# Tiles of the first two heads loaded in two steps, fourteen rows ahead of the last chunk's first write and two rows behind its last

## The reference, cut to what matters

```python
q, k, v = h @ wq.T, h @ wk.T, h @ wv.T             # per pixel, 512 -> 512 each
qkv = concat([q, k, v])                            # 1536 channels
dw = conv(qkv, dw_kernel, 5 x 5, one filter per channel)
pw = conv(dw, pw_kernel, 1 x 1, groups of 8 channels)
f = concat([qkv, pw]).reshape(B, 128, 24, N)       # 64 plain heads and 64 convolved ones
query, key, value = relu(f[:, :, :8]), relu(f[:, :, 8:16]), f[:, :, 16:]
scores = einsum('bhdn,bhen->bhde', value with a row of ones, key)
out = einsum('bhde,bhen->bhdn', scores, query)     # then divided by its last row
y = proj(out) * scale + shift + x
```

## Time and profile before

| | |
|---|---|
| median of 3 runs | 4719.41 us (4719.28 to 4723.08) |
| the profiled execution | 4729.61 us, of which 4727.8 us span |
| PE busy | 4394.5 us, 93% of the span |
| DVE, ACT, POOL busy | 2851.6, 2212.0, 1244.8 us |
| mean granted TensorE clock | 0.967 of full speed |
| attention (the phases described above) | about the first 2958 us of the span |

### The profile page before, as it was taken

One profiled execution on the slowest core, in us unless ns is written; L12 is line 12 of the kernel. 1 busy time (PEld: TensorE's weight loads), 2 busy tenths in 40 slices (PEclk: granted clock), 3 DMA queues, 4 the chain that ended last, 5 costly groups with the idle time before them and its releaser, 6 DMA issues. The chain is left out here.

```text
span 4727.8 us, 82817 instructions
## 1 busy us (share of the span) xinstructions
PE 4394.5 (93%) x30440; PEld 3543.8 (75%) x30440; DVE 2851.6 (60%) x4120; ACT 2212.0 (47%) x3983; POOL 1244.8 (26%) x1030
## 2 busy tenths in 40 slices
PE   8999999999999999999999999589989999999968
PEld 6887888888878878878888888466666676666626
DVE  4354454354454454544544544289789978978996
ACT  3343343343343433433433433056576666666666
POOL 2442432433433424424324333000030020002003
PEclk9999999999999999999999999799999999999989
DMA  6685685686776766856866767767456746746613
GB/s 195 222 290 200 234 289 203 240 274 214 245 241 222 265 226 235 285 199 234 288 205 225 265 218 236 267 213 246 163 197 216 248 145 209 253 158 203 204 54 126
DMA packets 486710, 1046.33 MB, mean 221 GB/s; under 512 B 40624, under 2 KB 94512, under 8 KB 484016
## 3 DMA queue, kind: packets, MB, share of 16 engines
q1 hardware_dynamic: 486320, 1040.99, 65.4%
HBM read 665.02 MB, written 375.82 MB: 220 GB/s over the span
## 5 line engine op out<-in xcount | busy, mean ns | idle before, releaser
L825 POOL TENSOR_TENSOR toeplitz<-taps 128x512 f32<-128x512 f32 x768 | 900.7, 1201 | 882.8 <-PE bank L488 804.0
L488 PEld LDWEIGHTS bank<-toeplitz,columns 128*128 128x128 f32 x8192 | 960.4, 193 | 15.1
L488 PE MATMUL bank<-toeplitz,columns 128*128 128x128 f32 x8192 | 960.1, 276 | 0.0
L394 PE MATMUL bank<-x_hi,w_hi 128*128 128x512 f32 x1536 | 619.0, 403 | 19.8 <-DVE x_lo L672 19.2
L396 PE MATMUL bank<-x_lo,w_hi 128*128 128x512 f32 x1536 | 603.9, 393 | 0.0
L395 PE MATMUL bank<-x_hi,w_lo 128*128 128x512 f32 x1536 | 603.9, 393 | 0.0
L1548 POOL TENSOR_TENSOR centred<-centred,x_out 128x512 f32<-128x512 f32 x128 | 174.4, 1384 | 1606.5 <-ACT centred L1331 1604.8
L759 DVE TENSOR_SCALAR ckey_t<-bank 128x256 f32<-128x256 f32 x256 | 108.6, 424 | 776.3 <-PE bank L488 776.3
L1181 PE MATMUL bank<-edge,w_branch 128*128 128x512 f32 x1024 | 485.8, 624 | 76.2 <-ACT edge L1279 76.2
L478 PE MATMUL bank<-loaded,toeplitz 128*128 128x256 f32 x2048 | 505.5, 391 | 53.6 <-DMA loaded<-tiles_dram 45.2
L672 DVE TENSOR_TENSOR x_lo<-x_sb,x_hi 128x1536 fp32r<-128x1536 f32 x128 | 251.8, 1967 | 426.6 <-ACT x_hi L543 426.6
(11 more groups left out here) (143 smaller groups left out, 6836.1 us busy)
## 6 DMA issues: line engine op xcount, KB each, us to landing
x_sb<-in_x_tiled SPq DMA_DIRECT2D x128, 1024.0 KB, 6.2
loaded<-tiles_dram SPq DMA_DIRECT2D x256, 433.5 KB, 5.8
tiles_dram<-tiles SPq DMA_DIRECT2D x112, 867.0 KB, 7.3
inverse<-inverse_dram SPq DMA_DIRECT2D x256, 256.0 KB, 7.9
att_dram<-out_hi SPq DMA_DIRECT2D x256, 256.0 KB, 4.4
att_dram<-out_lo SPq DMA_DIRECT2D x256, 256.0 KB, 5.7
att_hi<-att_dram SPq DMA_DIRECT2D x64, 1024.0 KB, 7.6
att_lo<-att_dram SPq DMA_DIRECT2D x64, 1024.0 KB, 10.0
```

Of the source, the lines that this page charges most:

```text
L394: nc.tensor.matmul(banks[t][:, :], wh, xh, start=(k == 0), stop=False)
L488: last = nc.tensor.matmul(bank[:, v * M:(v + 1) * M], columns[:, h % 2, t - T_K, v + b, a * HT:(a + TO) * HT], w[:, t, d, :], start=(d == ...
L825: last = nc.gpsimd.tensor_tensor(toeplitz[:, h % 2, t, :].rearrange("p (d o r) -> p d o r", o=HD, r=PL), tap, point, ALU.mult)
```

## The change

For heads 0 and 1 of each iteration (`EARLY_HEADS = 2`) the load is split by rows. Rows 0 to 13 (chunks 0 to 6) are loaded ahead of the last chunk's first write, behind a wait for the writes of all chunks up to the seventh (`load_early`). Rows 14 and 15 follow behind the last chunk's last write, each row of each head as a transfer of its own, since a row lies on 8 neighbouring partitions. For this the partitions of `loaded` are in the order (row, channel) in place of (channel, row), for all heads, and the taps are transposed on the host to match. The wait behind the last write is now for one semaphore. The spill that stood between the last write and the loads stands behind the loads. The two waits for a loaded head count the added transfers (`tile_loads`).

```diff
+        EARLY_HEADS = 2
+        FINAL = range(PL - PL // NCH, PL)
+
+        def tile_loads(it, h):
+
+            extra = len(FINAL) if h % LR < EARLY_HEADS else 0
+            return 16 * (SH // LR + extra) * it + 16 * (extra + h // LR + 1)
...
-                def load_head(h):
-
-                    sp.dma_start(loaded[:, h % LR, :, :].rearrange("p t s -> p (t s)"),
-                                 dram["tiles"][h * HD:(h + 1) * HD].rearrange("i r n -> (i r) n")
+                def load_head(h, of):
+
+                    sp.dma_start(loaded[of.start * HD:of.stop * HD, h % LR, :, :].rearrange("p t s -> p (t s)"),
+                                 dram["tiles"][h * HD:(h + 1) * HD, of, :].rearrange("i r n -> r i n")
                                  ).then_inc(tiles_loaded[h % LR], 16)
+
+                def load_early(it):
+                    for n in range(TB):
+                        writes = 1 if n == buffer(NCH - 1) else tile_writes(n)
+                        sp.wait_ge(tile_written[n], 16 * START + 16 * tile_writes(n) * it + 16 * writes)
+                    for h in range(EARLY_HEADS):
+                        load_head(h, slice(0, FINAL[0]))
...
+                        if j == NCH - 1:
+                            load_early(it)
                         write_tiles(it, j)
-                        if conv_of is not None and j >= LATE:
+                        if conv_of is not None and LATE <= j < NCH - 1:
                             spill(conv_of, 1, j - LATE)
...
-                    for n in range(TB):
-                        sp.wait_ge(tile_written[n], 16 * START + 16 * tile_writes(n) * (it + 1))
-
-                    for h in range(LR):
-                        load_head(h)
+                    n = buffer(NCH - 1)
+                    sp.wait_ge(tile_written[n], 16 * START + 16 * tile_writes(n) * (it + 1))
+
+                    for h in range(EARLY_HEADS):
+                        for r in FINAL:
+                            load_head(h, slice(r, r + 1))
+                    for h in range(EARLY_HEADS, LR):
+                        load_head(h, slice(0, PL))
+                    if conv_of is not None:
+                        spill(conv_of, 1, NCH - 1 - LATE)
...
-                    pe.wait_ge(tiles_loaded[h % LR], 16 * (SH // LR) * it + 16 * (h // LR) + 16)
+                    pe.wait_ge(tiles_loaded[h % LR], tile_loads(it, h))
...
+    tap = tap.transpose(1, 2, 0, 3, 4)
```

More of the change, by code:

```diff
@@ L312, in conv @@
                             sp.wait_ge(columns_ready, SH * it + h + 1)
-                            load_head(h + LR)
+                            load_head(h + LR, slice(0, PL))
                         if h % 2 == 1 and (h < SH - 3 or not last):
@@ L594, in gather @@
                 def gather(it, h):
-                    act.wait_ge(tiles_loaded[h % LR], 16 * (SH // LR) * it + 16 * (h // LR) + 16)
+                    act.wait_ge(tiles_loaded[h % LR], tile_loads(it, h))
                     if h >= 2:
```

## The result

The changed kernel takes 4756.78 us (median of 6 runs, 4744.10 to 4764.54) against 4721.24 us (6 runs, 4718.28 to 4731.30) for the kernel before in the same comparison: ratio 1.0067, 95% interval 1.0055 to 1.0078. It is 0.7% slower. The forecast was 4677 us, so the sign was wrong too. The profiled execution took 4756.03 us, 26.4 us more than that of before.

A forecast was written before the change was run, and what follows sets the result against it. PE, busy 93% of the span, was taken as the bound, waiting 45.2 us at conv's start for head 0's load. 4719.4 us less 24 (earlier start) and 18.5 (clock) gave 4677 us, range 4660 to 4705.

The forecast's parts named there:

- The new order of the rows slows every load: Rival, chance 0.05: in conv, loads landing later than 18.6 us cost 48 us per us beyond; 4744 at 20 us.
- What is late next: Step on conv's later heads, the moved spill, POOL and DVE: any delays there cost nothing.
- The sign that I gave for this rival: Loads within conv land after about 6 us; much more would speak for the slow-order rival.
- Whatever makes head 0 complete earlier moves PE by as much: At conv's start PE waits only for head 0's load, so it gains equally, up to 2.83 us a place.
- The early loads: Cost nothing: Ahead of the last chunk's writes: two issues of 0.44 us, data through by about 643, before the q write at 644.35.
- lost cover: If the early loads were not through in time, the q write would queue behind them, at most 1.9 us.
- the q write takes clearly over 2.7 us: Sign, at the last chunk's q write, that the early loads are in its way.
- The row transfer: Behind the last write: a 28 KB row lands in 1.9 us, completing head 0 after 2.3 us instead of 3.8.
- The clock: At conv's start: with PE idle only 1.3 us, the clock falls during the q matmuls are gone, 18.5 us gained.
- the clock still falls: Rival, chance 0.16: at conv's start the clock falls stay, only the 24 us term is left, 4695 us.
- The sum: Whole kernel: 24 + 18.5 = 42.5 us gained, from 4719.4 to 4677 us.
- -24 at the start: At conv's start: PE starts 1.5 us earlier in each of 16 places, 24 us in all.

The follow-up runs named there:

- experiment 1: The kernel before with only the loads' partition order changed to (row, channel), whole loads at their old places: 4777.9 us, ratio 1.0105 to the kernel before.
- experiment 4: The kernel before with loads in order (row, channel) at their old places, scratch stored as (row, channel, column): 4775.5 us, ratio 1.0108.
- experiment 5: The kernel before with its own order, an unused scratch row behind every eight, so each load reads 16 runs: 4788.2 us, ratio 1.0132.
- experiment 6: The kernel before with order (row, channel) read as one run, each chunk written in two transfers: 4763.5 us, ratio 1.0084.
- experiment 7: The kernel before with each load of taps issued one head earlier: 4720.6 us, ratio 0.9992.
- experiment 8: The changed kernel with each load of taps issued one head earlier: 4711.6 us, ratio 0.9972 to the kernel before.
- experiment 2: The kernel before with only the last spill moved behind the loads: 4733.4 us, ratio 1.0012.
- experiment 10: The changed kernel with the new order only in the two early heads and taps one head earlier: 4712.3 us, ratio 0.9979 to the kernel before.
- experiment 11: experiment 10 with PE's loop start moved from conv's start into plain, behind the last chunk's k and v matmuls: 4700.3 us, ratio 0.9958 to the kernel before.
- kernel 13: experiment 11 with one early head in place of two: 4690.7 us, ratio 0.9913 to the kernel before.
- experiment 12: experiment 7 with PE's loop start moved from conv's start into plain, no early loads: 4714.9 us, ratio 0.9982 to the kernel before.

## Why the prediction was wrong

**"The new order of the rows slows every load".** This is what turned the sign, through the step "What is late next". I had it as a rival with 0.05, saw the cause in the distance of 55,488 bytes, and let it decide only when a load took more than 18.6 us to land, since head 4 has that much room. Both were wrong. The cause is that the source isn't one run (experiments 1, 4, 5, 6). And the heads never were the ones to wait: all loads go through the same 16 engines, full in the middle of conv, and the transfer with the least room there is the taps' (experiments 7, 8). Less than 1 us a load, by the median, was enough for 52 us. The moved spill, which the same step put at nothing, costs 7 us by itself (experiment 2). The changed kernel is 18 us faster than experiment 1 by the ratios, so the load in two steps gave something back, but less than the order took. The trace of the kernel before had the full engines (1.03 to 1.05 from 676 to 706) and POOL's 78.7 us of waiting for taps; I read neither, because "What is late next" followed only the moved transfers and not what shares the engines with them. The sign that I gave for this rival couldn't have told it either: the whole loads of the changed kernel land after 6.1 us by the median (of the 128 whose landing the profile gives), the "about 6" of the forecast.

**"Whatever makes head 0 complete earlier moves PE by as much".** True in the first conv (2.38 to 1.30 us) and wrong behind a loop jump: PE's own sequencer was ready only just ahead of the load, and that was the next bound. In 5 of 16 places PE's wait ends with "issue", 12.8 us; what the jump adds over ACT's start is 7.4 us in all. Moving the loop's start gave 12 us (experiments 10, 11).

**"The early loads: Cost nothing".** I had them through by 643, ahead of the q write. They weren't, and the q write was held: by 1.4 us near 640 and by 0.8 us on the mean, 13 us in all, inside the 1.9 that I gave for lost cover. The term was mis-sized at its start: SP needed 1.79 us for the two issues (forecast 0.88), and near 640 the second load had landed 8.0 us after the first was issued, where I had 5.7. This is the recorded sign "the q write takes clearly over 2.7 us". Halving the early loads brings most of it back (experiments 11, 13). With the jump it closes the account of the idle time: 21.2 us forecast, 12.9 for the later q writes and 7.4 for the jump make 41.5. Measured were 39.0, since head 0 had been complete 3.9 us behind the write on the mean and not 3.8, and is now complete after 2.24 and not 2.3.

**The row transfer** was right: 1.76 us from issue to landing near 644 (forecast 1.9), the next one issued 0.33 to 0.35 us later (forecast 0.4), head 0 complete 2.15 us behind the landed write (forecast 2.3) and PE's matmul 2.26 us (forecast 2.4).

**The clock,** 18.5 us, was sized on an idle time of 1.3 us that didn't come about. The windows of the eight q matmuls sum to 43.11 us where they were 50.02, so 6.9 us came back; the clock falls in 9 of the 16, where it fell in 12. That is the rival "the clock still falls", for the greater part, at a wait that stayed at 2.4 us. The size of the term was right for the wait it was meant for: in kernel 13, whose mean wait is 1.4 us, the same eight matmuls take 33.9 us in all. Two windows of the changed kernel, the first and one behind a longer wait:

```profile
99.90:104.90 5.00, 1.97 (x8) 1.44 (x8) 1.00 0.90 202
462.30:467.30 5.00, 3.67 (x8) 2.52 (x8) 0.66 0.87 261
```

**The sum.** Forecast: -24 at the start, -18.5 clock. In the profiled execution: -6.2 idle at the start, -7.7 in head 0 (16 x 0.48, the clock), +35.7 in heads 7 to 10 (16 x 2.23), which makes 21.8; the rest of the 26.4, 4.6 us, I didn't trace. With all three hindrances taken away or halved, kernel 13 gains 0.87% of 4727.6, 41 us by its ratio (32 to 50 by its interval, 37 between the medians). That this lies close to the 42.5 of the forecast is partly luck: it holds the earlier taps and the moved loop too, worth 0.18% alone (experiment 12). Like for like, kernel 13 against kernel 12, the load in two steps is worth 0.69%, 33 us by the ratios (24 between the medians, from two chips), and in the profiled executions 15.9 us of idle time and 11.4 us of head 0. Some of kernel 13's gain is paid back in plain: PE waits there 12.6 us for "issue" at the loop's new start. So the mechanism was real, with 24 to 33 of the 42.5 us, and the change as made could not reach it.

**Left open:** why a source of 16 runs is slower with the same packets (how the transfer is laid on the engines isn't in these records); whether early loads smaller still, or issued earlier, give more; a place for PE's loop jump where it costs nothing; the changed kernel with the spill at its old place. None of these was tried.

## What to carry to other kernels

When a change makes every transfer of a kind a little slower, don't ask whether those transfers still have room; ask which transfer with the least room shares the engines with them in the stretch where they are full. When a wait is to be shortened, look up when the waiting engine's own next instruction is ready, above all at the start of a loop's body: a jump can lie hidden under the very wait that is removed. Moving bytes ahead of a critical write puts them in that write's way, so move the fewest that complete the first consumer's data.

## What the hardware showed unexpectedly

- A load of 433.5 KB to 128 partitions from 16 runs of 27,744 bytes, or from 128 rows of 3468 bytes in another order, lands in 4.0 to 4.5 us at the fastest, where one run lands in 3.0 to 3.1; the first two of an execution land 1.8 to 1.9 us apart instead of 1.1 to 1.5. Distance and order made no such difference (experiments 4, 5, 6).
- PE's jump to the start of its loop body takes effect some 3.8 us after it begins its last work ahead of it, and in the changed kernel PE starts up to 1.6 us behind the other reader of the same data for it.
- 27,744 bytes on 8 DMA engines land in 1.75 to 2.1 us; twice that in one transfer on 2 engines brings the head's completion some 2 us later than two transfers of half the size.
